# Column groups for one attention's weighted sum, and a new order of TensorE's and VectorE's work in the last two layers

## The reference

```python
# L2x: 16 heads of width 8; the 77 context rows are keys and values
q = (x @ Wq.T).reshape(B, Sq, H, Dh).transpose(0, 2, 1, 3)
k = (y @ Wk.T).reshape(B, -1, H, Dh).transpose(0, 2, 1, 3)
v = (y @ Wv.T).reshape(B, -1, H, Dh).transpose(0, 2, 1, 3)
attn = jax.nn.softmax(scores / sqrt(Dh), axis=-1)
out = jnp.einsum('bhqk,bhkd->bhqd', attn, v)
return out.transpose(0, 2, 1, 3).reshape(B, Sq, Dall) @ Wo.T + bo
# L3x: one head of width 128
scores = jnp.einsum('bqe,bke->bqk', Q, K) / scale
return jnp.einsum('bqk,bke->bqe', jax.nn.softmax(scores, axis=-1), V)
# L3f: each batch picks one of 8 experts by its mean row
scores = jnp.einsum('bh,he->be', x.mean(axis=1), Wr) + br
top1 = jnp.argmax(scores, axis=-1)
h = jax.nn.relu(jnp.einsum('bnh,bhf->bnf', x, W1[top1]) + b1[top1][:, None, :])
out = jnp.einsum('bnf,bfh->bnh', h, W2[top1]) + b2[top1][:, None, :]
```

## Time and profile before

| | us |
|---|---|
| median of 3 runs (lowest, highest) | 392.76 (392.56, 394.35) |
| the profiled execution's own time | 393.79 |
| its span | 392.1 |
| TensorE busy, of the span | 294.8 |
| VectorE busy | 221.9 |
| ScalarE busy | 135.7 |
| GpSimd busy | 103.8 |

### The profile page before, as it was taken

The page is one execution under the profiler, slowest core; times in us unless marked ns, Lnnn a source line. Parts: engine busy times, 40 slices in busy tenths (PEclk is TensorE's granted clock), DMA queues, the critical chain, the costliest instruction groups (busy, mean ns, idle before and its releaser), DMA issues.

```text
span 392.1 us, 4904 instructions
## 1 busy us (share of the span) xinstructions
PE 294.8 (75%) x1710; PEld 227.3 (58%) x1713; DVE 221.9 (57%) x614; ACT 135.7 (35%) x249; POOL 103.8 (26%) x100
## 2 busy tenths in 40 slices
PE   2789889999999936869993545869999255276496
PEld 1658779779999633338882132437888233155255
DVE  4445654801111158898954787697876598735401
ACT  1220243554433411334460711234363278111150
POOL 5700207712445411243351003133343100201100
PEclk9755955799999996989998555898999956555599
DMA  7970003469996130900000000000000000000001
GB/s 213 351 195 2 1 0 107 147 218 300 316 296 239 42 107 13 384 32 0 3 2 0 1 0 0 0 2 0 3 0 2 0 0 1 0 2 0 0 2 54
DMA packets 21399, 29.72 MB, mean 76 GB/s; under 512 B 3521, under 2 KB 14223, under 8 KB 21376
## 3 DMA queue, kind: packets, MB, share of 16 engines
q1 hardware_dynamic: 19686, 26.66, 21.6%
q0 software_dynamic: 1312, 2.60, 2.0%
q10 hardware_dynamic: 378, 0.16, 0.3%
HBM read 24.74 MB, written 4.67 MB: 75 GB/s over the span
## 4 chain that ended last, share of the span: by engine, by line
PE 55%; DVE 26%; ACT 6%; POOL 5%; issue 4%; DMA 2%; DVEq 0%; POOLq 0%; SPq 0%; ACTq 0%
PE bank L1052 9%; PE bank L994 5%; PE bank L819 5%; PE bank L1002 5%; PE bank L1036 3%; DVE ln L1233 3%; POOL rstd L507 3%; PE bank L860 3%; DVE bn L1225 3%; PE bank L1034 3%; PE bank L1198 2%; DVE pr L1449 2%; PE bank L1207 2%; DVE pmax L1448 2%; DVE psums L1457 1%
## 5 line engine op out<-in xcount | busy, mean ns | idle before, releaser
L507 POOL TENSOR_TENSOR rstd<-var,minus_half 128x4 f32<-128x4 f32 x16 | 16.2, 1013 | 146.8 <-DVE var L1230 146.6
L532 POOL TENSOR_TENSOR pr<-pr,psums 128x1232 f32<-128x1232 f32 x12 | 27.0, 2248 | 54.3 <-DVE psums L1459 54.3
L574 ACT ACTIVATE prT<-bank 128x512 f32<-128x512 f32 (+1 forms) x48 | 22.2, 488 | 50.7 <-PE bank L819 50.4
L792 PE MATMUL bank<-ident,ln 128*128 128x128 f32 x40 | 9.6, 385 | 29.9 <-DVE ln L1233 29.9
L1448 DVE TENSOR_REDUCE pmax<-bank 128x6 f32<-128x462 f32 (+1 forms) x48 | 27.5, 573 | 7.4 <-PE bank L1038 5.3
L550 POOL DMA_INDIRECT yt<-acc,pr x23 | 22.0, 957 | 33.0 <-DVE acc L1432 30.4
L819 PE MATMUL bank<-ident,pr 128*128 128x128 f32 (+1 forms) x140 | 22.2, 293 | 8.3 <-POOL pr L532 7.9
L1233 DVE TENSOR_SCALAR ln<-x,mv,rstd 128x128 f32<-128x128 f32 x56 | 19.0, 443 | 15.9 <-POOL rstd L507 15.9
L1432 DVE COPY acc<-bank 128x128 f32<-128x128 f32 x23 | 6.7, 292 | 37.5 <-PE bank L1002 37.5
L1034 PE MATMUL bank<-m,lnT 128*128 128x462 f32 (+1 forms) x48 | 23.3, 625 | 3.2 <-DVE pr L1449 1.7
L792 PEld LDWEIGHTS bank<-ident,ln 128*128 128x128 f32 x40 | 6.3, 194 | 32.9 <-issue 30.6
(11 more groups left out here) (293 smaller groups left out, 628.6 us busy)
## 6 DMA issues: line engine op xcount, KB each, us to landing
experts<-in_w SPq DMA_DIRECT2D x23, 512.0 KB, 4.6
experts<-in_w SPq DMA_DIRECT2D x2, 2048.0 KB
xg<-pr SPq DMA_DIRECT2D x1, 1518.0 KB, 9.6
pr<-xg SPq DMA_DIRECT2D x5, 264.0 KB, 6.0
experts<-yt SPq DMA_DIRECT2D x4, 256.0 KB, 3.6
x<-in_x SPq DMA_DIRECT2D x2, 256.0 KB, 3.9
wkv<-in_wk SPq DMA_DIRECT2D x1, 512.0 KB, 6.6
wkv<-in_wv SPq DMA_DIRECT2D x1, 512.0 KB, 6.5
```

Source lines behind the costliest of these rows:

```text
L507: pool.tensor_tensor(rstd[:, b * TB:b * TB + TB], var[:, b, :], minus_half[:, :], ALU.pow).then_inc(rstd_ready, 1)
L532: pool.tensor_tensor(v, v, psums[:, n % 4, 1, :].unsqueeze(2).to_broadcast([P, H, R]), ALU.mult).then_inc(p_ready, 1)
L574: ins = act.activation(dst[:, c0:full, :], bank[:, 0:(full - c0) * P].rearrange("p (c k) -> p c k", k=P), ACT.Copy)
```

## The change

Three edits:

1. `weighted` of L2x computes its 128 output columns as four groups q of 32 (four heads each), each in its own 32 partitions of the bank and its own 32 columns of the array. Group q needs only the chunks that hold its heads: 3, 3, 4 and 3 of the ten. That is 13 matmuls of 32 weight columns instead of 10 of 128, ordered so that consecutive ones are of different groups.
2. L3x: both bias rows go ahead of everything; then transposes and scores of batch 0, then of batch 1.
3. L3f: transposes and router of a batch follow each other. VectorE picks batch 0's expert before it scales batch 1's rows; `pick_ready` is raised after the copies of `w1s` and `b1s`, and a new semaphore `pick2_ready`, waited for ahead of the second matmuls, after `w2s` and `b2s`.

```diff
+QH = H // 4
+QD = D // 4
+QCH = [list(range(q * QH * R // P, ((q + 1) * QH * R - 1) // P + 1)) for q in range(4)]
...
-                    for c in range(CH):
-                        k = min(P, HR - c * P)
-                        w, v = prT[0:k, n % 2, c, :], (n1 if layer == "L1x" else v2)[0:k, n // TB, c, :]
-                        l, r = (w, v) if layer == "L1x" else (v, w)
-                        ins = pe.matmul(o, l, r, start=(c == 0), stop=(c == CH - 1))
+                    if layer == "L1x":
+                        for c in range(CH):
+                            k = min(P, HR - c * P)
+                            ins = pe.matmul(o, prT[0:k, n % 2, c, :], n1[0:k, n // TB, c, :],
+                                            start=(c == 0), stop=(c == CH - 1))
+                    else:
+                        for i in range(max(len(cs) for cs in QCH)):
+                            for q, cs in enumerate(QCH):
+                                if i < len(cs):
+                                    c = cs[i]
+                                    k, d = min(P, HR - c * P), slice(q * QD, q * QD + QD)
+                                    ins = pe.matmul(o[d, :], v2[0:k, n // TB, c, d], prT[0:k, n % 2, c, :],
+                                                    start=(i == 0), stop=(i == len(cs) - 1))
...
-            for b in range(B):
-                transpose_rows("L3x", b)
-            for b in range(B):
+            def key_bias(b):
                 bank = acquire(S, ("s3", b))
-                pe.wait_ge(*lnT_done("L3x", b))
                 pe.matmul(bank[:, 0:TB * R].rearrange("p (t r) -> p t r", t=TB), ones[0:1, :],
                           cb3[:, b * R:b * R + R].unsqueeze(1).to_broadcast([1, TB, R]), start=True, stop=False)
+
+            def scores_3(b):
+                bank = S.bank(("s3", b))
+                pe.wait_ge(*lnT_done("L3x", b))
...
+            for b in range(B):
+                key_bias(b)
+            for b in range(B):
+                transpose_rows("L3x", b)
+                scores_3(b)
...
+            pe.wait_ge(*loaded("l3f"))
             for b in range(B):
                 transpose_rows("L3f", b)
-            pe.wait_ge(*loaded("l3f"))
-            for b in range(B):
                 bank = acquire(S, ("pick", b))
...
                 bank = acquire(O, ("L3f", b))
+                pe.wait_ge(pick2_ready, b + 1)
...
-            for b in range(B):
-                update(("L3x", b), b, 3)
-                normalise("L3f", b)
...
+            def copy_chosen(b):
                 e = dve.value_load(top3i[0:1, b, 0:1], min_val=0, max_val=E - 1)
                 dve.tensor_copy(w1s[:, b, :], ex_flat[:, bass.ds(e * (2 * FF), FF)])
+                dve.tensor_copy(b1s[:, b, :], b1_flat[:, bass.ds(e * C, C)]).then_inc(pick_ready, 1)
                 dve.tensor_copy(w2s[:, b, :], ex_flat[:, bass.ds(e * (2 * FF) + FF, FF)])
-                dve.tensor_copy(b2s[:, b, :], b2_flat[:, bass.ds(e * D, D)])
-                dve.tensor_copy(b1s[:, b, :], b1_flat[:, bass.ds(e * C, C)]).then_inc(pick_ready, 1)
+                dve.tensor_copy(b2s[:, b, :], b2_flat[:, bass.ds(e * D, D)]).then_inc(pick2_ready, 1)
+
+            for b in range(B):
+                update(("L3x", b), b, 3)
+                statistics("L3f", b)
+                if b == 0:
+                    less_mean("L3f", b)
+            dve.wait_ge(*loaded("l3f"))
+            choose(0)
+            less_mean("L3f", 1)
+            copy_chosen(0)
+            choose(1)
+            copy_chosen(1)
```

More of the change, by code:

```diff
@@ L374, in program @@
         pick_ready = sem("pick_ready")
+        pick2_ready = sem("pick2_ready")
         biased = sem("biased")
@@ L1220, in step, with statistics @@
                 dve.wait_ge(dve_step, steps[0])
-            def normalise(layer, b, out=ln):
+            def statistics(layer, b):
                 for t in range(b * TB, b * TB + TB):
@@ L1230, in normalise, with less_mean @@
                 dve.tensor_scalar(var[:, b, :], mv[:, b * TB:b * TB + TB, 1], EPS, None, ALU.add).then_inc(var_ready, 1)
+            def less_mean(layer, b, out=ln):
                 dve.wait_ge(rstd_ready, var_done(layer, b)[1])
@@ L1235, in normalise @@
                 ins.then_inc(ln_ready, 1)
+            def normalise(layer, b, out=ln):
+                statistics(layer, b)
+                less_mean(layer, b, out)
             def update(key, b, gate, src=None):
@@ L1580, in _, with choose @@
                 softmax_out(b, B + b + 1)
-            for b in range(B):
-                update(("L3x", b), b, 3)
-                normalise("L3f", b)
-            dve.wait_ge(*loaded("l3f"))
-            for b in range(B):
+            def choose(b):
                 key = ("pick", b)
```

## The result

The changed kernel takes 380.74 us in the median of four runs (379.81 to 381.1), the kernel before 393.56 (392.56 to 394.42) beside it. The ratio is 0.9691, 95% interval 0.9652 to 0.973: faster, by 12.8 us between the medians. The forecast was 381.2 in a range of 378.8 to 386.0.

What follows compares the result with a forecast made beforehand. TensorE was taken to bound the second attention by under 0.9 us, the order of work the last two layers. Gains of 6.4 + 3.8 + 1.8 = 12.0 gave a median of 380.8, plus 0.4 for the clock 381.2; range 378.8 to 386.

Steps and rivals of the forecast that it cites:

- The bound: Second attention's step: TensorE bounds it by under 0.9 us; after the change TensorE needs 4.87, VectorE 5.05 and is late.
- One sign: L2x step after the change: 5.05 to 5.1 us, with TensorE's busy share below 1 and VectorE's near it.
- The block, 1.16 forecast: L2x weighted sum up to the next transposes: eight passes 0.86 plus 0.30 for switching width, 1.16 instead of 2.24 us.
- Row groups: At line 860 records of two row groups ran side by side; the same was taken for column groups.
- Half overlap: Rival for the weighted sum: 13 pairs advance by 0.107 each, block 1.69, time 383.2 with the clock's 0.4; chance 0.14.
- no overlap: Rival for the weighted sum: one moving stream at a time, block 3.08, time 394; chance 0.08.
- A switch at each change of group: Rival for the weighted sum: array empties whenever the group changes, block 4.8, time 408; chance 0.08.
- The stage, 6.4 forecast: L2x: VectorE's update comes at 300.25 instead of 306.62, gain 6.4 of 8.6 us spared; 2.2 become waits.
- L3x, 3.8 forecast: L3x: batch 1's scores start at 344.65 and are read 2.03 later, at 346.68 instead of 350.50; gain 3.8 us.
- L3f, 1.8 and -0.4 forecast: L3f: expert matmuls start right behind batch 1's router, gain 1.8 us; 0.4 added to the time for the clock.
- the clock's term: L3f: TensorE's clock may rise up to 3 us later relative to the expert matmuls' start; 0.4 us added.
- The sum of 11.6: Whole kernel: gains 6.4 + 3.8 + 1.8 = 12.0 us, with 0.4 taken off for the clock in L3f.

Runs made afterwards that it cites:

- one_group: Changed kernel with all 13 matmuls of the weighted sum sent to one column group; 406.29 us beside 405.53 for the kernel before, ratio 1.0024.
- two_groups: Changed kernel with the weighted sum in two groups of 64 columns, 11 matmuls; 382.7 us, ratio 0.9713 to the kernel before.
- in_pairs: Changed kernel with groups 0 and 1 in turn until complete, then groups 2 and 3; 395.36 us beside 406.92 for the kernel before, one run.
- order_only: Changed kernel with the four-group weighted sum undone, the L3x and L3f edits kept; 401.21 us, ratio 0.9891 to the kernel before.
- late_router: Changed kernel with batch 1's router matmul behind the first expert matmul of batch 0; 378.0 us, one run.
- one_chunk: Changed kernel computing only each group's first chunk, four matmuls instead of 13, so another result; 380.36 us, ratio 0.9654 to the kernel before.
- group_by_group: Changed kernel with the 13 matmuls written one group after the other; 398.69 us, ratio 0.9791 to the kernel before.
- two_and_two: Changed kernel with the 13 matmuls in runs of two of one group; 378.57 us, one run.
- batch_order: Changed kernel with L3x's second half (softmax, transposes, outputs) batch by batch; 378.54 us, one run.

## Why the prediction was right

**The bound.** Right. TensorE set the step before, and with a shorter weighted sum VectorE sets it: its reductions lie back to back, and TensorE waits for GpSimd's tile, which waits for VectorE's inverse. One sign failed to show: TensorE's busy share stays at 1 in the window from 274.83 to 279.70 and falls below it only in the next step. The margin of under 0.9 us is what kept 8 x 1.1 us of spared work from being 8 x 1.1 of gain.

**The block, 1.16 forecast.** It was 1.01 from its first record to the next transposes. To that comes the entry, which lies ahead of the first record. In the kernel before, the last two transposes start 0.21 ahead of the weighted sum (281.88 in the earlier trace rows and the row below, of its timeline), after it is 0.31 (274.52 to 274.83):

```profile
281.67 0.38 PE L819 MATMUL bank<-ident,att_all 128*128 128x128 f32 x2
```

The entry of 0.10 and the block of 1.01 make 1.11, so 1.13 are spared, not 1.08. Its parts: first to last start 0.80 (0.86 forecast for eight passes; it is seven distances, and one more pass stands behind the last start), 0.10 in (0.12), and 0.20 from the last start to the transposes, 0.09 over a plain distance of 0.11 (0.18 forecast). Row groups were a good guide to column groups, and the 0.09 of the earlier trace rows was the right price of a change of width; the 0.16 beside it was too high. *Half overlap* (1.69) and *no overlap* (3.08) are out by the starts. one_group, which has no overlap by construction, took 2.96 + 0.10 = 3.06. *A switch at each change of group* is out: neighbours of different groups start 7 ns apart. Here the Trainium skill's rule that changing the tile doesn't drain (TensorEngine Tiling (Array Packing), "Key Properties") agrees with the trace. Its 2.38x for three groups, with 512 moving columns (TensorE: Matmul & The Clock Gate, "Measured speedup vs the span model") doesn't carry over: four groups here take 801 ns from first to last start where one takes 2760, 3.4x, of the 25/7 = 3.6x that the distances of all records over those of the longest group would allow.

**The stage, 6.4 forecast, 7.1 measured.** The right mechanism with two terms a little off. VectorE's step was 4.98 and 4.91, not 5.05. The first reduction of a step took 0.64 where VectorE had stood idle just before it, as in the earlier trace rows, and 0.57 where it came straight from the inverse; so in all fourteen traces, but for 0.62 once (two_groups) and 0.59 once (in_pairs). And it starts 0.08 before the inverse's record ends (278.53 against 278.61). The last inverse but one ends at 288.42 (288.8 forecast), GpSimd hands over its last tile at 292.96 (293.4), tile 7 starts at 293.11 (293.55), and from there to the update it is 6.33 (6.68), with two shorter sums in it. The second of these, which starts behind a wait for ScalarE, is worth 1.42 and not 1.08: from its start to ScalarE's copy it was 2.53 (302.11 to 304.64) and is 1.11 (296.36 to 297.47). 0.44 and 0.35 are the 0.8 by which 299.44 is ahead of 300.25.

**L3x, 3.8 forecast.** Right: 339.55 is 2.02 behind the start of batch 1's scores (2.03 forecast), and order_only has the stage of the changed kernel.

**L3f, 1.8 and -0.4 forecast.** The 1.8 is right, and for the reason given: the pick fits with 0.36 to spare, and TensorE waits for its own router. late_router shows this: with the router moved, the matmuls start 1.2 earlier although the copies are as late as before. The sign of the clock's term was wrong. The clock rose 3.0 us behind the first expert matmul instead of 4.0, which gave 0.5 us where I had taken 0.4 off. In the kernels here that distance is 2.8 to 5.0 us, and the last layer follows it at half its length. In the twelve traces without the moved router the rest of the layer is 18.29 + half of what the distance has over 3.01, within 0.02. What sets the distance isn't settled; no run here varied it alone.

The sum of 11.6 stands against 13.2: 0.7 of the difference is L2x, 0.9 the clock. That the time came out only 0.5 under the forecast is in part luck: the median of the kernel before stood 0.8 higher in its four runs (393.56) than in the three that the forecast starts from (392.76).

## What to carry to other kernels

A matmul that needs only a part of its output columns for each part of its sum can be split over 32-column groups of the array; four groups ran at the pace of one here, in fp32. Write the groups in turn, or in short runs: three waiting records of a group (an fp32 matmul is two) hold nothing up, the fourth holds up all.

Before costing such an edit, read what the next engine needs for a step. Here VectorE was 0.9 us behind TensorE, and of 9.0 us of spared TensorE time 7.1 came through; one_chunk spared 8 x 0.63 = 5.0 more (its block is 0.38) and got 0.7, with a fallen clock.

In a stretch where all engines wait in turn, look at what stands ahead of the awaited instruction in its own queue. Four such moves gave 1.2 to 3.8 us each on the path, and none of them took work away.

## What the runs showed of the hardware

- Each column group of TensorE has room of its own for three waiting records. Records of one group start 109 ns apart with 128 moving columns; a record of a free group starts 5 to 8 ns behind the one before it where one waiting record stands between them in the program, or 13 where three do. Starts thus leave the program's order: in group_by_group, as counted, a record of the second group starts ahead of three of the first. In two_and_two the program's last record, which raises the semaphore, is even the 24th of 26 to start, and by its record it ends 0.19 us before the last one does. The semaphore still rises behind that last one: 1.118 us after the first start in the first sum, 30 ns behind the end of the last record, and so in all eight sums; where the last record of the program is also the last to start, it rises 14 ns behind its end. So in these runs the semaphore of the last matmul covered the records of other groups that started after it. (Ends of matmuls are modelled, the semaphore's rise is an event of the trace.)
- The change from 128 to 32 weight columns costs 0.10 us, and back 0.09.
- TensorE's clock at the end of the program rose 2.8 to 5.0 us behind the first expert matmul in the fourteen traces, which differ mostly ahead of it. A gain of 1 to 2 us there can be halved or given back by it, as in late_router and batch_order, and is judged by stage.
